# Cross attention with the softmax sums beside the values, and the feed-forward's last gate and up columns in one block

## The reference, cut to what matters

```
scores = where(causal, einsum('bhqd,bhkd->bhqk', qh, kh) / 4, min)     # 16 heads of 16 channels
attn   = softmax(scores, axis=-1)
out    = einsum('bhqk,bhkd->bhqd', attn, vh)  ->  out @ Wout.T
...
h      = silu(x @ w_gate) * (x @ w_up)        # all experts' 1408 columns, and 704 of the shared one
y      = sum over experts of combine * (h @ w_down) + sigmoid(x @ g) * shared
```

## Time and profile before

| | |
|---|---|
| median of 3 runs (lowest, highest) | 670.1 us (669.79, 672.28) |
| profiled execution: its own time, its span | 672.13 us, 670.4 us |
| mean granted clock over the span | 0.992 |
| busy in the span: TensorE, VectorE, GpSimd, ScalarE | 620.8, 381.1, 343.2, 269.3 us |
| group 0 to its third norm's transposes; groups 1, 2, 3 and the tail | up to 144.6; to 298.1, 452.1, about 592, 670.4 us |

### The profile page before, as it was taken

The page is one execution under the profiler, slowest core; times in us unless marked ns, Lnnn a source line. Parts: engine busy times, 40 slices in busy tenths (PEclk is TensorE's granted clock), DMA queues, the critical chain, the costliest instruction groups (busy, mean ns, idle before and its releaser), DMA issues.

```text
span 670.4 us, 16277 instructions
## 1 busy us (share of the span) xinstructions
PE 620.8 (93%) x6728; PEld 498.1 (74%) x6728; DVE 381.1 (57%) x780; ACT 269.3 (40%) x608; POOL 343.2 (51%) x474
## 2 busy tenths in 40 slices
PE   7987956799999899999999899999999999999996
PEld 6444444445889799755888899854798889899996
DVE  6797778768734454769642544769752444552220
ACT  4957123132335555242335545341325545243332
POOL 7674164214455655614455565615364555508666
PEclk9989989899999999999999999999999999999999
DMA  8911000010121111002031121002021111014220
GB/s 193 361 52 33 1 1 2 1 50 17 40 72 37 41 51 42 11 23 59 26 86 27 37 56 41 21 16 66 22 52 32 37 49 48 22 37 126 65 69 17
DMA packets 41540, 34.15 MB, mean 51 GB/s; under 512 B 9613, under 2 KB 40918, under 8 KB 41466
## 3 DMA queue, kind: packets, MB, share of 16 engines
q1 hardware_dynamic: 39562, 31.27, 17.5%
q10 hardware_dynamic: 1904, 1.84, 0.8%
HBM read 30.92 MB, written 2.17 MB: 49 GB/s over the span
## 4 chain that ended last, share of the span: by engine, by line
PE 45%; DVE 21%; POOL 14%; ACT 8%; issue 8%; DMA 2%; SPq 0%; ACTq 0%; POOLq 0%; DVEq 0%
PE bank L984 7%; DVE A L1451 6%; DVE nm L1528 4%; PE bank L988 4%; PE bank L989 3%; PE bank L990 3%; POOL hb L597 3%; POOL hT_last L685 3%; POOL A L677 3%; PE bank L1161 3%; PE bank L1233 3%; PE bank L1090 3%; ACT A L866 2%; PE bank L1023 2%; PE bank L1079 2%
## 5 line engine op out<-in xcount | busy, mean ns | idle before, releaser
L1426 DVE TENSOR_TENSOR hb<-hb,bank 128x256 f32<-128x256 f32 x102 | 42.7, 419 | 144.5 <-ACT hb L759 144.2
L597 POOL TENSOR_TENSOR hb<-hb,cwb 128x256 f32<-128x256 f32 x102 | 76.2, 747 | 79.6 <-DVE hb L1426 79.5
L587 POOL TENSOR_TENSOR hT<-hb,hT 128x256 fp32r<-128x256 f32 x102 | 79.4, 778 | 73.1 <-ACT hT L749 73.1
L749 ACT ACTIVATE hT<-hb 128x256 fp32r<-128x256 f32 x102 | 42.4, 416 | 122.6 <-POOL hb L597 122.1
L988 PE MATMUL bank<-xTf,wGh 128*128 128x256 f32 x272 | 82.7, 304 | 0.0
L1451 DVE TENSOR_TENSOR A<-bank,decay 128x512 f32<-128x512 f32 x128 | 77.5, 682 | 8.3 <-PE bank L1079 8.1
L989 PE MATMUL bank<-xTf,wUh 128*128 128x256 f32 x272 | 76.8, 282 | 0.0
L989 PE MATMUL bank<-xTf,wGh 128*128 128x256 f32 x272 | 76.8, 282 | 0.0
L990 PE MATMUL bank<-xTf,wGl 128*128 128x256 f32 x272 | 76.6, 282 | 0.0
L988 PE MATMUL bank<-xTf,wUh 128*128 128x256 f32 x272 | 76.6, 281 | 0.0
L990 PE MATMUL bank<-xTf,wUl 128*128 128x256 f32 x272 | 76.5, 281 | 0.0
(11 more groups left out here) (216 smaller groups left out, 1401.7 us busy)
## 6 DMA issues: line engine op xcount, KB each, us to landing
cwb<-cw_rows SPq DMA_DIRECT2D x54, 128.0 KB, 2.9
A<-cw_rows SPq DMA_DIRECT2D x18, 128.0 KB, 3.4
A<-in_x SPq DMA_DIRECT2D x4, 512.0 KB, 4.4
res<-in_x SPq DMA_DIRECT2D x4, 512.0 KB, 4.5
out_x<-res SPq DMA_DIRECT2D x8, 256.0 KB, 2.4
rawG<-in_L_ffn_w_gate SPq DMA_DIRECT2D x2, 704.0 KB, 6.7
rawU<-in_L_ffn_w_up SPq DMA_DIRECT2D x2, 704.0 KB, 7.1
cwb<-cw_rows SPq DMA_DIRECT2D x12, 112.0 KB, 2.8
```

Of the source, the lines that this page charges most:

```text
L587: pool.tensor_tensor(hT[:, c % 2, 1, :], hb[:, c % 2, :], hT[:, c % 2, 0, :].bitcast(F32), ALU.subtract).then_inc(h_lo, 1)
L597: pool.tensor_tensor(hb[:, c % 2, :], hb[:, c % 2, :], cwb[:, c % CWS, :], ALU.mult).then_inc(h_scaled, 1)
L749: act.activation(hT[:, c % 2, 0, :], hb[:, c % 2, :], ACT.Copy).then_inc(h_hi, 1)
L1426: tt(hb[:, c % 2, :], hb[:, c % 2, :], PS[5 + c % 2][:, HT:GT], ALU.mult).then_inc(gu_used, 1)
```

## The change

`xvp` holds ones where it held zeros, and `onesp` is gone. A product with it now gives in one go a head's 16 output rows and, in the other 16 rows, its sum 16 times. The products of w = 0 and w = 1 are not accumulated any more: w = 0 goes to the left half of the bank, w = 1 to the right half. So outputs and sums of the two heads stand crosswise, and are sorted: ScalarE copies the left half twice with a 0/1 column `xcol` as its scale (`first_heads`), once into the sums' tile (the rows of the other head) and once into `yT`; VectorE adds the right half times the other column to both (`second_heads`); `attended` takes the reciprocal of the sums in place, swaps the two 16-row halves of each 32 partitions by a shuffle, and multiplies. `sums_of` gives the tile: `rec`, and `hb[:, 0]` for the odd batches of group 0. The waits on `yT_ready` that meant that the bank is read become `o_taken`; the out projection's first half waits for two batches, its second for four.

In groups 1 to 3 `attended(b)` moves from the end of batch b to batch b+1, between its exponentials and the ticks of `xbc`; `layer_stats` moves to batch 0, `layer_rstd(0)` to batch 0 ahead of the ticks of `xbc`, and `layer_apply` is split in two pairs, after the ticks of batch 1 and of batch 2. In group 0 the order is as the diff shows.

In the feed-forward the last 64 up columns are loaded behind the last 64 gate columns, and block 16 is one block of 64 gate and 64 up columns: `gate_up` makes 6 matmuls for it in place of 12, Silu reads partitions 0 to 63 and the product reads the up part from partitions 64 to 127; all that follows works on 64 partitions (`hidden`), `down` too. The zero pads are gone. GpSimd's share of the low parts of the gate weights grows by 64 columns, that of the up weights shrinks by 64.

The diff, cut: left out are the semaphores' names and count, the same edit with `hidden` in `ffn_tick`, `silu_last`, `product_last`, `scale_last`, the last group's high and low parts, the wait for three loads in `split_high`, and `first_heads(b)`, `first_heads(b + 1)` behind each pair's exponentials in group 0.

```diff
+def sums_of(g, b):
+    return hb[:, 0, :] if g == 0 and b % 2 else rec
+SWAP = list(range(XD, 2 * XD)) + list(range(XD))
...
 SB = SI // P
-FW = [(wGh, wGl, rawG, 0), (wGh, wGl, rawG, 1), (wUh, wUl, rawU, 0), (wUh, wUl, rawU, 1)]
+NU = (FB - 1) * P
+FW = [(wGh, wGl, rawG, 0, FP), (wGh, wGl, rawG, 1, FP), (wUh, wUl, rawU, 0, NU), (wUh, wUl, rawU, 1, NU)]
...
-        hi, lo, raw, k = FW[n]
-        w = slice(FCUT, NF) if pool_side else slice(0, FCUT)
+        hi, lo, raw, k, width = FW[n]
+        w = slice(FCUT, width) if pool_side else slice(0, FCUT)
...
+def packed(n):
+    return n % FB == FB - 1
+def hidden(n):
+    return slice(0, P // 2) if packed(n) else slice(0, P)
+def up_part(bank, n):
+    return bank[P // 2:P, 0:HT] if packed(n) else bank[:, HT:GT]
 def split_hi(n):
     if n < 4:
-        hi, lo, raw, k = FW[n]
-        return hi[:, k, 0:NF], raw[:, k, 0:NF]
+        hi, lo, raw, k, width = FW[n]
+        return hi[:, k, 0:width], raw[:, k, 0:width]
...
             sp.dma_start(raw[:, k, 0:NR].rearrange("p (e i) -> p e i", e=E), we[:, ks, :].rearrange("e p i -> p e i")).then_inc(f_in[2 * w + k], 16)
-            sp.dma_start(raw[:, k, NR:NF], ws[ks, :]).then_inc(f_in[2 * w + k], 16)
+            if w == 0:
+                sp.dma_start(raw[:, k, NR:NF], ws[ks, :]).then_inc(f_in[k], 16)
+                sp.dma_start(raw[:, k, NF:FP], sw_up[ks, NU - NR:SI]).then_inc(f_in[k], 16)
+            else:
+                sp.dma_start(raw[:, k, NR:NU], ws[ks, 0:NU - NR]).then_inc(f_in[2 + k], 16)
...
                             pattern=[[-1, P]], channel_multiplier=1))
-    made(pool.memset(onesp[:], 0.0))
-    for w in range(2):
-        made(pool.memset(onesp[:, w, XD * w:XD * w + XD], 1.0))
...
     decay_cut_half(1)
-    for t in (wGh, wGl, wUh, wUl):
-        pool.memset(t[:, :, NF:FP].bitcast(F32), 0.0).then_inc(pads, 1)
...
-        pool.tensor_tensor(hT[:, c % 2, 1, :], hb[:, c % 2, :], hT[:, c % 2, 0, :].bitcast(F32),
+        hr = hidden(n)
+        pool.tensor_tensor(hT[hr, c % 2, 1, :], hb[hr, c % 2, :], hT[hr, c % 2, 0, :].bitcast(F32),
...
             other = slice(XD, 2 * XD) if w == 0 else slice(0, XD)
-            pool.memset(xvp.rearrange("p b (h w) n -> p (b h) w n", w=2)[:, :, w, other], 0.0).then_inc(xvp_zero, 1)
+            pool.memset(xvp.rearrange("p b (h w) n -> p (b h) w n", w=2)[:, :, w, other], 1.0).then_inc(xvp_ones, 1)
         if g == 0:
-            pool.wait_ge(w_tp, 9)
-            pool.wait_ge(xvp_zero, 2)
-            for t in (wDh, wDl):
-                pool.memset(t[64:P, FB - 1, :].bitcast(F32), 0.0).then_inc(pads, 1)
-            pool.wait_ge(pads, 6)
+            pool.wait_ge(xvp_ones, 2)
...
                                    pattern=[[0, 4], [1, T]], channel_multiplier=-1).then_inc(p_ready, 1)
-            if b == 0 and g == 0:
+            if b == 0 and g + 1 < NG:
                 layer_rstd(0, g + 1)
             point(g, f"x{b}c")
-            if b == 1 and g + 1 < NG and g:
-                layer_rstd(0, g + 1)
...
             act.wait_ge(down_done, c - 1)
-        act.activation(hT[:, c % 2, 0, :], hb[:, c % 2, :], ACT.Copy).then_inc(h_hi, 1)
+        act.activation(hT[hidden(n), c % 2, 0, :], hb[hidden(n), c % 2, :], ACT.Copy).then_inc(h_hi, 1)
...
+        def first_heads(b):
+            act.wait_ge(o_part, g * 4 + b + 1)
+            if g and b:
+                act.wait_ge(yT_ready, g * 4 + b)
+            elif g == 0 and b >= 2:
+                act.wait_ge(yT_ready, b - 1)
+            src = PS[attend_bank(g, b)][:, 0:2 * P]
+            act.activation(sums_of(g, b), src, ACT.Copy, scale=xcol[:, 1:2]).then_inc(o_copied, 1)
+            act.activation(yT[:, :, b * T:(b + 1) * T], src.rearrange("p (m t) -> p m t", m=KC), ACT.Copy, scale=xcol[:, 0:1]).then_inc(o_copied, 1)
...
                 point(g, f"x{b}c")
+                first_heads(b)
...
             if n == 0 and g:
-                pe.wait_ge(yT_ready, g * 4)
+                pe.wait_ge(o_taken, g * 4)
...
         for a, wh, wl in ((0, wGh, wGl), (HT, wUh, wUl)):
+            if a and packed(n):
+                break
...
         h2 = hT[:, c % 2] if f < NG - 1 else hT_last[:, n % LAST_HT]
-        hi, lo = h2[:, 0, :], h2[:, 1, :]
+        hr = hidden(n)
+        hi, lo = h2[hr, 0, :], h2[hr, 1, :]
...
-            mm(o, hi[:, t], wDh[:, j, :], start=(j == 0 and b == 0), stop=False, skip_group_check=True)
-            mm(o, hi[:, t], wDl[:, j, :], start=False, stop=False, skip_group_check=True)
-            last = mm(o, lo[:, t], wDh[:, j, :], start=False, stop=j == FB - 1, skip_group_check=True)
+            mm(o, hi[:, t], wDh[hr, j, :], start=(j == 0 and b == 0), stop=False, skip_group_check=True)
+            mm(o, hi[:, t], wDl[hr, j, :], start=False, stop=False, skip_group_check=True)
+            last = mm(o, lo[:, t], wDh[hr, j, :], start=False, stop=j == FB - 1, skip_group_check=True)
...
                         pe.wait_ge(*ready[k])
+                    elif done is wout_ready and k == 0:
+                        pe.wait_ge(yT_ready, g * 4 + 4)
...
                     if i == 0:
-                        pe.wait_ge(yT_ready, g * 4 + b - 1)
+                        pe.wait_ge(o_taken, g * 4 + b - 1)
...
             if b and g:
-                pe.wait_ge(yT_ready, g * 4 + b)
+                pe.wait_ge(o_taken, g * 4 + b)
             for m in range(2):
-                for s in range(2):
-                    for w in range(2):
-                        for i in range(4):
-                            v = xvp[:, b, 8 * m + 2 * i + w, :] if s == 0 else onesp[:, w, :]
-                            a = (2 * s + m) * T
-                            last = mm(PS[attend_bank(g, b)][32 * i:32 * i + 32, a:a + T], v, weights_of(g, b)[:, i, (2 * m + w) * T:(2 * m + w + 1) * T],
-                                      start=w == 0, stop=w == 1, skip_group_check=True)
+                for w in range(2):
+                    for i in range(4):
+                        a = (2 * w + m) * T
+                        last = mm(PS[attend_bank(g, b)][32 * i:32 * i + 32, a:a + T], xvp[:, b, 8 * m + 2 * i + w, :],
+                                  weights_of(g, b)[:, i, (2 * m + w) * T:(2 * m + w + 1) * T], start=True, stop=True, skip_group_check=True)
             last.then_inc(o_part, 1)
...
         point(g, "y0")
-        pe.wait_ge(yT_ready, g * 4 + 4)
-        out_projection(yT, [(yT_ready, g * 4 + 4), (yT_ready, g * 4 + 4)], wX[:, 1], (0, 1), wout_ready)
+        if g == 0:
+            pe.wait_ge(o_taken, 3)
+        out_projection(yT, [(yT_ready, g * 4 + 2), (yT_ready, g * 4 + 2)], wX[:, 1], (0, 1), wout_ready)
...
-    def layer_apply(s, g, src, dst):
+    def layer_apply(s, g, src, dst, batches=range(GB)):
         i = 0 if s == 0 else 1
         dve.wait_ge(ln_rstd[s], g + 1)
-        for b in range(GB):
+        for b in batches:
...
+        def second_heads(b):
+            src, sums, y3 = PS[attend_bank(g, b)][:, 2 * P:4 * P], sums_of(g, b), yT[:, :, b * T:(b + 1) * T]
+            dve.wait_ge(o_copied, (g * 4 + b) * 2 + 2)
+            stt(sums, src, xcol[:, 0:1], sums, ALU.mult, ALU.add).then_inc(sums_ready, 1)
+            stt(y3, src.rearrange("p (m t) -> p m t", m=KC), xcol[:, 1:2], y3, ALU.mult, ALU.add).then_inc(o_taken, 1)
         def attended(b):
-            dve.wait_ge(o_part, g * 4 + b + 1)
-            if b:
-                dve.wait_ge(yT_ready, g * 4 + b)
-            nc.vector.reciprocal(rec, PS[attend_bank(g, b)][:, 2 * P:4 * P]).then_inc(rec_ready, 1)
+            sums, y3 = sums_of(g, b), yT[:, :, b * T:(b + 1) * T]
+            dve.wait_ge(sums_ready, g * 4 + b + 1)
+            nc.vector.reciprocal(sums, sums).then_inc(rec_ready, 1)
             dve.wait_ge(rec_ready, g * 4 + b + 1)
-            tt(yT[:, :, b * T:(b + 1) * T], PS[attend_bank(g, b)][:, 0:2 * P].rearrange("p (m t) -> p m t", m=KC),
-               rec.rearrange("p (m t) -> p m t", m=KC), ALU.mult).then_inc(yT_ready, 1)
+            nc.vector.stream_shuffle(sums, sums, SWAP).then_inc(rec_swapped, 1)
+            dve.wait_ge(rec_swapped, g * 4 + b + 1)
+            dve.wait_ge(o_taken, g * 4 + b + 1)
+            tt(y3, y3, sums.rearrange("p (m t) -> p m t", m=KC), ALU.mult).then_inc(yT_ready, 1)
...
             point(g, "x0a")
+            second_heads(0)
+            second_heads(1)
             attended(0)
-            attended(1)
             maxima(2)
             maxima(3)
             layer_apply(0, g + 1, tokx, tokx)
+            attended(1)
             point(g, "x2a")
+            second_heads(2)
+            second_heads(3)
             attended(2)
...
                 point(g, f"x{b}b")
-                if b == 1 and g + 1 < NG:
+                if b:
+                    attended(b - 1)
+                elif g + 1 < NG:
                     dve.wait_ge(x_in, 16 * (g + 2))
                     layer_stats(0, g + 1, tokx)
-                if b == 2 and g + 1 < NG:
```

(7 more changed lines are left out.)

43 lines of the change are left out of this document (25 added, 18 removed).

## The result

| | kernel before | changed kernel |
|---|---|---|
| median of 6 runs (lowest, highest) | 671.19 us (669.30, 674.19) | 676.96 us (674.76, 677.79) |
| ratio, 95% interval | | 1.0076 (1.0050, 1.0101) |
| profiled execution's span | 670.4 us | 676.1 us |
| mean granted clock | 0.992 | 0.967 |

The forecast was 666.5 us in a range of 661.5 to 671.5. It had the wrong sign, and the time lies outside the range.

A forecast was written before the change was run, and what follows sets the result against it. Two chains of equal length, TensorE's own and one through VectorE and ScalarE, bound the kernel. Terms -3.6-0.15+2.8+3.7+1.4 gain 4.2 us, taking 670.1 to 665.9; 0.6 for the clock makes 666.5, range 661.5 to 671.5.

The forecast's parts named there:

- the charge for the clock: Ends of groups 1 and 2: a clock fall costs up to 1.2 us each; 0.6 us charged at even chance for one.
- tick 33: Feed-forward, groups 1 and 2: packed, this tick ends before a wait, so its saving was counted as worth nothing.
- (5): Rival: the clock falls at the ends of both groups 1 and 2, giving 668.3 us; chance 0.14.
- Group 0 loses: Group 0's cross attention: TensorE waits there, so the saving hides nothing of VectorE's new work; 3.6 us lost.
- +0.4: Group 0: copies, additions and `attended(0)` before `maxima(2)` move it from 101.62 to 102.0 us.
- the chains in groups 1 to 3: Batch to batch, the chain beside TensorE's decides; gains 0.87, 1.06, 0.55 us in groups 1 and 2, 1.2, 1.05, 1.08 in group 3.
- The idle place for `attended`: Groups 1 to 3: moved to where VectorE waits 5.04 us for the Silu, its 2.6 us are hidden.
- rivals 2 and 3: VectorE's new parts cheaper or better hidden, 658 to 664 us, chance 0.17; or the shuffle dear, 674 us, chance 0.08.
- Rival 3: Dear shuffle: each 0.1 us costs 0.6; gain gone from 1.6 us, over 0.5% slower above 1.8; chance 0.08.
- Rival 4: Halved `attend` keeps its time or ScalarE holds the ticks; groups give nothing, 670 to 671 us; chance 0.12.
- The end of the stage: Groups 1 and 2, last batch: longer `attended` has no cover, so the transposes come 1.1 us later after its maximum.
- the tail: From 608 us to the end: both packed blocks lie ahead of GpSimd's last idle, gaining 2x0.72 = 1.4 us.

The follow-up runs named there:

- e13_fill2: Changed kernel with matmuls nobody reads in TensorE's waits of groups 0 to 2, most in group 0; 670.41 us, ratio 0.9999 to the kernel before.
- e8_before_fill: Kernel before with matmuls nobody reads between group 0's `attend`s and ahead of the third norm's transposes of groups 0 to 2; 670.06 us, ratio 0.9972.
- e2_ones: Changed kernel without the packed block, its new attention kept; 680.09 us, ratio 1.0113 to the kernel before.
- e15_order0_fill: Changed kernel with unread matmuls in TensorE's waits and group 0's `attended(0)` and `attended(2)` ahead of the next batch's additions; 667.49 us, ratio 0.9954.
- e10_order: Changed kernel's order and packed block with the old form of attention in every batch; 671.33 us, ratio 0.9993 to the kernel before.
- e11_form: Changed kernel with old attention in group 0 and every group's last batch, and the order of before in groups 1 to 3; 685.38 us, ratio 1.0205.
- e1_packed: Kernel before with only the packed block added, attention unchanged; 672.68 us, ratio 1.0012 to the kernel before.
- e6_hybrid_fill: Changed kernel with old attention in group 0 and every group's last batch, plus unread matmuls in group 0's waits; 661.33 us, ratio 0.9852.
- e9_fill_all: Changed kernel, old attention in group 0 and last batches, unread matmuls in group 0's waits and ahead of groups 1 and 2's transposes; 661.79 us, ratio 0.9852.
- e16_norecip: Changed kernel with unread matmuls in TensorE's waits, without reciprocal and shuffle for batches 2 and 3 of group 0; 667.04 us, ratio 0.9940.

## Why the prediction was wrong

**The step that failed is the charge for the clock.** The prediction put 0.6 us for "an even chance for one of them", of two groups. Both paid, 1.52 and 1.18 us (e13_fill2 against the changed kernel), so 2.7 for 0.6. And group 0, for which the prediction charged nothing beyond the 1.2 that its `attend(1)` had lost before, paid 3.14 where the kernel before paid 2.33 (e8_before_fill). By these executions that is 3.5 more than before for 0.6 charged; 2.7 of it are firm. The prediction had the row (an idle of 3.26 with a clock at 1.2 GHz behind it) and had worked out that TensorE has less to do in group 0, but did not put the two together. With 32 records fewer for each batch and the same waits TensorE was at 1.2 GHz at 88 to 103 and at 109 to 123 us; before, in this attention, at 95 to 99. Part of the idle time at the groups' ends comes from the packed block, whose tick 33 the prediction called "worth nothing": 2.67 us in the changed kernel are 1.98 in e2_ones, though the clock fell in both. Of the rivals, (5) "both clocks fall" described groups 1 and 2 rightly, and none had the clock down through group 0. The Trainium skill (TensorE: Matmul & The Clock Gate, "HAM oscillation") describes such a clock that falls again and again, with the cost paid each time, for waits on DMA of about 3 to 5 us. The trace agrees that it is paid again and again, but behind shorter gaps (1.97 to 2.69 us at all ten group ends that had them); the prediction used that rule for the groups' ends alone.

The clock does not account for the miss by itself: with 2.9 more charged the forecast would have been 669.4, still under the 670.1 of before and inside the range. It takes the next steps to turn the sign.

**The second step is "Group 0 loses", 3.6 forecast.** With unread matmuls on both sides it is 121.33-116.20 = 5.1. M(2) is at M(0)+20.2 in e13_fill2 and at M(0)+18.9 in e8_before_fill: 1.3 where "+0.4" was forecast. That figure had compared with an M(2) that stood late behind an `attend` at 1.2 GHz, so the slow clock of before hid a part of VectorE's new work. The other 3.8 are the forecast's own: the additions wait for the last copies, and 5.2 us of `attended` follow (120.89 to 126.09). The comparison of e15_order0_fill with e13_fill2 shows that 2.2 of the 5.1 are a matter of place: `attended` of the even batches belongs in front of the additions of the odd ones.

The whole miss in the profiled execution is 9.25 us (+5.70 against -4.15 with 0.6 charged): clock 3.5-0.6 = 2.9, start 1.75, group 0's work 1.5, groups 1 and 2 with the clock held 0.53 and 1.01, group 3 and the tail 1.5, which adds up to 9.2. The start is chance, so 1.75 of the profiled miss is luck; the division between clock and work in group 0 rests on single executions.

**Right: the chains in groups 1 to 3.** M to M was forecast as 15.7, 17.2, 16.0 and came as 15.93, 17.34, 16.33. The idle place for `attended` and the fact that TensorE's saving counts only partly are borne out by e10_order and e11_form. **Right, a size off:** the copies take 0.47 us, started 0.37 apart (forecast 0.37 and 0.3), the additions 0.48, started 0.40 apart (0.34). That is 0.2 to 0.3 for each batch, the 0.64 us by which M(0) to M(3) missed. The shuffle took 0.44 with 0.01 for its mask (0.5), and the reciprocal from SBUF 1.75, as kept; so rivals 2 and 3 are out. (Rival 3's own sum was wrong: at 0.6 us for each 0.1, a shuffle of 1.1 to 1.2 us, and not 1.6, would have taken the gain, and one of 1.7 made the kernel slower by 0.5%.) Rival 4 had the groups giving nothing, which is near what groups 1 and 2 did, but not for its reason: `attend` was halved, and the gain was there at M(3), 1.84 us, and lost behind it. **Right: the end of the stage.** Transposes at M(3)+28.03 (27.9), idle 2.67 (about 3). What it costs was put at 1.1 and is 1.4 with the clock held (102.07 to 103.48).

**Wrong in the tail, 1.4 forecast, 0.65 to 0.74 measured.** The prediction let "a fixed row of GpSimd work" follow GpSimd's last idle and carried 2x0.72 through to the end unreduced. In the kernel before that idle ends at M(3)+98.15, 13.4 us before the end; in e1_packed at M(3)+95.87, 15.0 before the end:

```profile
658.70 0.73 POOL L698 TENSOR_TENSOR hT_last<-A,hT_last 128x256 fp32r<-128x256 f32 x1 [0.71 <-ACT hT_last L930]
```

This is one tick earlier in the list than the last idle before, so the two rows are not the same tick. Compared tick by tick the two packed blocks each brought their 0.72: in e1_packed GpSimd goes from 0.16 late to 0.56 early at the first, and from 0.15 to 0.87 early (97.28 for 98.15) at the second. Between them 0.39 was lost, where GpSimd waited 1.09 us and not 0.69 for ScalarE, and TensorE's matmuls beside the first block's `down` started 0.20 to 0.23 apart four times instead of 0.12. Behind the second, where GpSimd is never idle, another 0.22 went, most of it in the last 6.7 us. So the term was mis-sized by what the engines around the packed blocks lost again, not by the blocks.

**The start.** Nothing in the change explains its +1.90. Of 18 profiled executions nine have M(0) at 80.1 to 80.8 us, and nine at 81.4 to 83.9; each of the nine late ones has a stretch at 1.2 GHz at 36 to 42 us, and none of the others. e6_hybrid_fill (80.37) and e9_fill_all (83.67) have the same instructions up to there, and the same idle times of TensorE before it (1.19 and 0.76 us); the clock fell in one and not in the other. So it is chance as far as the program goes. How much of the spread of every version's runs it makes is not shown, as only one execution of each was profiled. What tips it stays open.

## What to carry to other kernels

Work taken from TensorE beside a wait is not free: it leaves a longer idle engine, and the clock can fall for everything that follows. Price it at every place where the removed work stood next to a gap, and try matmuls that nobody reads in those gaps before judging the change; here they were worth 6 of 677 us. See to it that they are short enough: in e16_norecip they were themselves what the next work waited for. A form that moves work from TensorE to VectorE pays only in the batches that have a wait of VectorE to hide it in (here three of four, and no group without the feed-forward beside it), so use it there alone. A saving ahead of a wait is not worth nothing: it makes the wait longer, and that has its own price. And as the clock falls or stays by chance behind one and the same gap, profile a version more than once before giving a microsecond a cause.

## What had not been expected of the hardware

A copy of 128x256 from PSUM on ScalarE took 0.37 us plain and 0.47 with a column as its scale. The reciprocal of 128x256 took 1.75 us from PSUM and from SBUF alike, four times a product. The shuffle of 128x256 took 0.44 us. The length of an idle time did not decide by itself whether the clock fell. Before the third norm's transposes of groups 1 and 2, over all versions that show the wait, it fell behind all ten idle times of 1.97 to 2.69 us, behind three of ten of 1.15 or 1.16, and behind none of twelve of 0.28 to 0.52; at the residual's wait in batch 1 it stayed up behind eight of eleven of 1.68 to 1.95. And the stretch before M(0) came out 0.6 to 3.8 us longer in half of the profiled executions, in e9_fill_all for the same instructions as in e6_hybrid_fill.
